# Normalised rows stored as two fp16 pieces and read back by transposing DMAs, in an attention and mixture-of-experts kernel on one core

## What is computed

```python
# x, ctx: 16 x 128 x 512, fp32.  D = 512 columns.
ln(x)  = (x - mean) / sqrt(var + 1e-5)
# cross attention per sample: 8 heads of 16 rows, over the 128 x 512 matrices
qk = einsum('hdq,hdl->hql', ln(x) heads, ctx heads) / 4
a  = einsum('hql,hdl->hdq', softmax(qk), ctx heads) * gamma
x1 = x + tanh(g_xattn) * a
u  = ln(x1)                                    # the "normalised rows"
# expert layer on u: 2048 tokens of 512
h = u @ down_w + down_b                        # 256 columns
logits = u @ router_w + router_b - cost        # 8 experts, the two best
out = sum over both of gate * (gelu(gelu(h) @ w1 + b1) @ w2 + b2)
out += 0.1 * (gelu(gelu(h) @ shared_w1 + shared_b1) @ shared_w2 + shared_b2)
out = out @ up_w + up_b + gelu(u) @ core_w + core_b
result = x1 + tanh(g_ffn) * out
```

## Time and profile before

| | |
|---|---|
| median of 3 runs | 705.38 us (704.84 to 709.47) |
| the profiled execution | 702.09 us, span 699.5 us from first to last instruction |
| busy share of the span | PE 94%, ACT 76%, DVE 73%, POOL 67% |
| chain that ended last, by engine | PE 65%, POOL 13%, DMA 11%, ACT 3%, DVE 3% |
| DMA | 120.40 MB, mean 172 GB/s |

### The profile page before, as it was taken

How to read it: one execution, slowest core, us unless ns; L and a number is a source line. 1 busy time by engine, 2 the same in 40 slices (tenths; PEclk the granted TensorE clock), 3 DMA queues, 4 the chain that set the end, 5 groups by cost and what they waited for, 6 DMA issues and landing times.

```text
span 699.5 us, 18429 instructions
## 1 busy us (share of the span) xinstructions
PE 655.4 (94%) x6005; PEld 344.4 (49%) x6005; DVE 512.5 (73%) x859; ACT 531.0 (76%) x1125; POOL 466.8 (67%) x468
## 2 busy tenths in 40 slices
PE   1799999999999999999999998879999999999998
PEld 0122222222222222222364554469889999998744
DVE  3989999999999999999779657554343343344466
ACT  2389999999999999999886747447677777777411
POOL 3698998988989888886658441405665665665722
PEclk9999999999999999999999999999999999999999
DMA  6655776666766666555254752459987997696596
GB/s 204 240 167 187 223 247 200 189 197 187 218 205 203 219 195 193 193 160 191 85 152 163 266 183 78 159 138 170 131 138 116 118 139 113 95 120 95 61 296 252
DMA packets 128482, 120.40 MB, mean 172 GB/s; under 512 B 64132, under 2 KB 97668, under 8 KB 128392
## 3 DMA queue, kind: packets, MB, share of 16 engines
q1 hardware_dynamic: 114968, 104.09, 51.7%
q0 software_dynamic: 12192, 14.16, 13.5%
q10 hardware_dynamic: 1232, 0.98, 0.5%
HBM read 60.25 MB, written 49.10 MB: 156 GB/s over the span
## 4 chain that ended last, share of the span: by engine, by line
PE 65%; POOL 13%; DMA 11%; ACT 3%; DVE 3%; issue 2%; SPq 1%; another core or an unknown queue 1%; POOLq 0%; DVEq 0%
PE EH L1333 24%; PE Y L1333 15%; PE pv L571 11%; PE ring L558 7%; PE nat L546 4%; ACT P L642 2%; DMA rd<-den_scratch 2%; DMA k_scratch<-khl 2%; POOL wlo L812 2%; DMA u<-in_wall 2%; DMA q_scratch<-qhl 1%; POOL tn L746 1%; POOL y_sums L2231 1%; POOL khl L804 1%; POOL whi L808 1%
## 5 line engine op out<-in xcount | busy, mean ns | idle before, releaser
L717 DVE TENSOR_REDUCE mx<-nat 128x2 f32<-128x1024 f32 x256 | 296.2, 1210 | 14.5 <-PE nat L546 14.3
L642 ACT ACTIVATE P<-ring 128x512 f32<-128x512 f32 x512 | 281.1, 601 | 16.2 <-PE ring L558 10.2
L2231 POOL DMA_INDIRECT y_sums<-ysb,to x74 | 123.2, 1665 | 92.5 <-DVE ysb L2165 73.6
L571 PE MATMUL pv<-P,VT 128*32 128x256 f32 x2048 | 157.9, 392 | 0.4
L546 PE MATMUL nat<-KS,QS 48*128 48x512 f16 x512 | 113.1, 395 | 21.1 <-DMA QS<-q_scratch 15.1
L558 PE MATMUL ring<-QS,KS 49*128 49x512 f16 x512 | 119.0, 391 | 8.0 <-ACT P L642 6.8
L1333 PE MATMUL EH<-XA,whi 128*128 128x256 f16 (+1 forms) x688 | 104.8, 258 | 0.0
L1333 PE MATMUL Y<-whi,u 128*128 x592 | 104.0, 273 | 0.1
L571 PEld LDWEIGHTS pv<-P,VT 128*32 128x32 f32 x2048 | 44.0, 108 | 99.3 <-issue 49.3
L2115 DVE TENSOR_TENSOR u<-X,u 128x512 f16<-128x512 f32 x62 | 42.6, 689 | 62.1 <-ACT u L1739 61.7
L1333 PE MATMUL EH<-XA,wlo 128*128 128x256 f16 (+1 forms) x344 | 84.7, 258 | 0.0
(11 more groups left out here) (282 smaller groups left out, 1029.3 us busy)
## 6 DMA issues: line engine op xcount, KB each, us to landing
QS<-q_scratch SPq DMA_DIRECT2D x64, 96.0 KB, 2.9
KS<-k_scratch SPq DMA_DIRECT2D x62, 96.0 KB, 2.3
u<-in_wall SPq DMA_DIRECT2D x7, 640.0 KB, 4.0
X<-in_x SPq DMA_DIRECT2D x16, 256.0 KB, 3.5
q_scratch<-qhl SPq DMA_DIRECT2D x16, 256.0 KB, 2.1
xr<-in_x SPq DMA_DIRECT2D x16, 256.0 KB, 3.4
rd<-den_scratch SPq DMA_DIRECT2D x16, 256.0 KB
u_rows<-un SPq DMA_DIRECT2D x16, 256.0 KB
```

The source lines that it names most:

```text
L571: m = pe.matmul(pv[32 * j:32 * j + 32, q], VT[i][:, lb, g, j, :], Pb[4 * (s % 2) + j][:, q], start=(lb == 0 and half == 0), stop=(lb == 3) ...
L642: act.activation(Pb[4 * (s % 2) + j][:, :], bank[:, :], ACT.Exp).then_inc(t_use.sem, 1)
L717: dve.tensor_reduce(mx[:, k // 8, :, k % 8], nat[k % 2][:, :, :], AX.X, ALU.max).then_inc(t_max.sem, 1)
L2231: pool.indirect_dma_start(out=ysum[:, :], out_offset=bass.IndirectOffsetOnAxis(ap=to[:, j % 2, a:a + 1], axis=0), in_=ysb[j % 2][:, a, :], ...
```

## The change

Attention now writes `u` as two fp16 pieces: after `u` (L766, into a spare buffer) GpSimd makes `uhi` and `ulo`, and SP stores both to a `u_rows` of two halves. `load_u(r)` becomes two transposing DMAs, of the high and of the low pieces, straight into the places that `h` reads: `uh` and `ul` for odd groups, the two halves of `XA` for even ones. `uT` (TensorE), `uT` and `uh` (ScalarE), `ul` (VectorE), the four casts `uhp` (GpSimd) disappear. `uf` is now the sum of both pieces, four adds on VectorE at the head of each body; `lg` and `gu` wait for it. `load_u(3)` moves from before the stores of group 0's residual rows to behind `sums(0)`, ahead of `load_x(2)`. The core of the diff:

```diff
--- before.py
+++ after.py
@@ -178,7 +179,7 @@
-    us = nc.dram_tensor("u_rows", [B, P, L], F32, kind="Internal").ap()
+    us = nc.dram_tensor("u_rows", [2, B, P, L], F16, kind="Internal").ap()
@@ -255,7 +258,8 @@
-    un = A("un", [P, L])
+    uhl = A("uhl", [P, 2, L], F16)
+    un = lambda b: gap[0][:, 0, :] if b < B - 3 else u[:, :, :].rearrange("p t q -> p (t q)")[:, UN_AT:UN_AT + L]
@@ -348,7 +352,7 @@
-            jobs += [(w - 3, n) for n in ("xnegm", "xveps", "xrstd", "u", "x1t")]
+            jobs += [(w - 3, n) for n in ("xnegm", "xveps", "xrstd", "u", "uhi", "ulo", "x1t")]
@@ -489,8 +493,8 @@
-                ck.wait(t_pool, s, "u")
-                sp.dma_start(us[s], un[:, :]).then_inc(t_us.sem, 16)
+                ck.wait(t_pool, s, "ulo")
+                sp.dma_start(us[:, s].rearrange("h p q -> p h q"), uhl[:, :, :]).then_inc(t_us.sem, 16)
@@ -762,8 +766,14 @@
+                done(pool.tensor_scalar(un(b), ao[i][:, :], lnx[:, 0:1], lnx[:, 2:3], ALU.add, ALU.mult))
+            elif what == "uhi":
+                ck.wait(t_pool, b, "u")
-                done(pool.tensor_scalar(un[:, :], ao[i][:, :], lnx[:, 0:1], lnx[:, 2:3], ALU.add, ALU.mult))
+                done(pool.tensor_scalar(uhl[:, 0, :], un(b), 1.0, 1.0, ALU.mult, ALU.mult))
+            elif what == "ulo":
+                ck.wait(t_pool, b, "uhi")
+                done(pool.tensor_tensor(uhl[:, 1, :], un(b), uhl[:, 0, :], ALU.subtract))
@@ -868,7 +878,7 @@
-        eng.wait_ge(t_pool.sem, t_pool.at[B + 1, "wlo"])
+        eng.wait_ge(t_pool.sem, max(t_pool.at[B + 1, "wlo"], t_pool.at[B - 4, "ulo"]))
@@ -961,9 +971,12 @@
-    xb, ub = [X, XB, X, XB], [XA, XA, u, XA]
+    xb = [X, XB, X, XB]
+    even = flat(XA).bitcast(F16).rearrange("p (h k q) -> p h k q", h=2, k=LB)
+    high_of = lambda r: uh[:, :, :] if r % 2 else even[:, 0]
+    low_of = lambda r: ul[:, :, :] if r % 2 else even[:, 1]
@@ -1025,17 +1038,17 @@
-                "pe": four("uT") + [("lg", 0), ("lt", 0), ("h", 0), ("h", 1), ("rk", 0), ("rt", 0), ("rt", 1), ("gt", 0), ("rt", 2), ("rt", 3)],
+                "pe": [("lg", 0), ("lt", 0), ("h", 0), ("h", 1), ("rk", 0), ("rt", 0), ("rt", 1), ("gt", 0), ("rt", 2), ("rt", 3)],
-                "dve": four("uf") + [("lpc", 0)] + four("ul") + R_(["lred", "lb", "lmx", "lsub", "lcl"] + route_a + route_s + route_p) +
+                "dve": four("uf") + [("lpc", 0)] + R_(["lred", "lb", "lmx", "lsub", "lcl"] + route_a + route_s + route_p) +
-                "pool": four("uhp") + four("sc"),
+                "pool": four("sc"),
-            ahead = cur(four("uT")) + older([("y", 1)]) + old([("a", 0), ("a", 1)]) + \
+            ahead = older([("y", 1)]) + old([("a", 0), ("a", 1)]) + \
@@ -1044,7 +1057,7 @@
-            ahead = cur([(n, k) for k in range(LB) for n in ("uT", "uh")]) + old([("a", 0), ("sah", 0)]) + cur([("lg", 0)]) + \
+            ahead = old([("a", 0), ("sah", 0)]) + cur([("lg", 0)]) + \
@@ -1052,7 +1065,7 @@
-            ahead = cur(four("ul")) + old([("sal", 0)]) + cur(R_(["lred", "lb", "lmx", "lsub", "lcl"] + route_a)) + low(0) + \
+            ahead = cur(four("uf")) + old([("sal", 0)]) + cur(R_(["lred", "lb", "lmx", "lsub", "lcl"] + route_a)) + low(0) + \
@@ -1174,11 +1183,14 @@
-            if r in (1, 3):
-                wait(sp, t_pe, (0, 0, 0, 1)[r], "uT", LB - 1)
-            elif r == 2:
-                sp.wait_ge(t_z.sem, 4)
-            sp.dma_start(ub[r][:, :, :], us[r * G4:(r + 1) * G4].rearrange("t p q -> p t q")).then_inc(t_uu[r % 2].sem, 16)
+            if r == 1:
+                ends["stacks"](sp)
+            elif r >= 2:
+                wait(sp, t_pe, r - 2, "h", 1)
+                wait(sp, t_dve, r - 2, "uf", LB - 1)
+            for h, dst in enumerate((high_of(r), low_of(r))):
+                rows_ = us[h, r * G4:(r + 1) * G4].rearrange("t p q -> (t p) q")
+                sp.dma_start_transpose(dst, rows_).then_inc(t_uu[r % 2].sem, 16)
@@ -1224,7 +1236,6 @@
-            load_u(3)
@@ -1245,6 +1256,7 @@
+                    load_u(3)
@@ -1368,28 +1379,20 @@
-                if name != "uT":
-                    wait(pe, t_act, 0, "uT", early[0, name, i])
-            if name == "uT":
-                if i == 0:
-                    wait(pe, t_uu[r % 2], r)
-                for t in range(G4):
-                    m = pe.transpose(dst[:, t * P:t * P + P], ub[r][:, t, i * P:i * P + P], ident)
-            elif name == "lg":
+            if name == "lg":
-                    wait(pe, t_act, r, "uT", k)
+                    wait(pe, t_dve, r, "uf", k)
+                if i == 0:
+                    wait(pe, t_uu[r % 2], r)
-                    if i == 0:
-                        wait(pe, t_act, r, "uh", k)
-                        wait(pe, t_dve, r, "ul", k)
-                    m = three(dst, slice(c0, c0 + P), uh[:, k, :], ul[:, k, :], k == 0, k == LB - 1)
+                    m = three(dst, slice(c0, c0 + P), high_of(r)[:, k, :], low_of(r)[:, k, :], k == 0, k == LB - 1)
@@ -1526,13 +1529,8 @@
-        def rows_0(lo, hi):
-            if lo == 0:
-                ends["scores"](pe)
-            for k in range(lo, hi):
-                do(0, "uT", k)
-
+            ends["scores"](pe)
@@ -1599,14 +1597,7 @@
-            if name == "uT":
-                wait(act, t_act, r - 1, "guh", i)
-                wait(act, t_dve, r - 1, "gul", i)
-                m = act.copy(uf[:, i, :], src)
-            elif name == "uh":
-                wait(act, t_pe, r - 1, "h", 1)
-                m = act.copy(uh[:, i, :], bank(r, "uT", i))
-            elif name == "lg":
+            if name == "lg":
@@ -1619,9 +1610,8 @@
-                wait(act, t_dve, r, "ul", i)
+                wait(act, t_dve, r, "uf", i)
-                wait(act, t_act, r, "uT", i)
@@ -1996,17 +1986,15 @@
-                wait(dve, t_pe, 0, "uT", i)
-                m = dve.tensor_copy(uf[:, i, :], bank(0, "uT", i))
+                if i == 0:
+                    wait(dve, t_uu[r % 2], r)
+                wait(dve, t_act, r - 1, "guh", i)
+                wait(dve, t_dve, r - 1, "gul", i)
+                m = dve.tensor_tensor(uf[:, i, :], high_of(r)[:, i, :], low_of(r)[:, i, :], ALU.add)
-            elif name == "ul":
-                wait(dve, t_act, r, "uT", i)
-                wait(dve, t_act, r, "uh", i)
-                wait(dve, t_pe, r - 1, "h", 1)
-                m = dve.tensor_tensor(ul[:, i, :], uf[:, i, :], uh[:, i, :], ALU.subtract)
```

More of the change, by code:

```diff
@@ L57 @@
 R_MAX = K_QK
+UN_AT = 2 * NT * 16
 HALF = 64
@@ L230, in attention @@
     wst = [v[:, :, :].rearrange("p t q -> p (t q)") for v in (XA, u)]
+    gap = []
     def stacks(i):
         if i:
-            A("gap", [P, 3, L])
+            gap.append(A("gap", [P, 3, L]))
         own = [A(f"{n}{i}", [P, 2, QUADS // 2, L], F16) for n in ("QS", "KS")]
@@ L518, in last_u @@
         def last_u():
-            sp.wait_ge(t_pool.sem, t_pool.at[B - 1, "u"])
-            sp.dma_start(us[B - 1], un[:, :]).then_inc(t_us.sem, 16)
+            sp.wait_ge(t_pool.sem, t_pool.at[B - 1, "ulo"])
+            sp.dma_start(us[:, B - 1].rearrange("h p q -> p h q"), uhl[:, :, :]).then_inc(t_us.sem, 16)
         late["sync"] = last_x1, last_u
@@ L832, in last_norm @@
         def last_norm():
-            for what in ("xnegm", "xveps", "xrstd", "u", "x1t"):
+            for what in ("xnegm", "xveps", "xrstd", "u", "uhi", "ulo", "x1t"):
                 job(Clock(pool), B - 1, what)
@@ L1070, in ffn @@
         t_xx[r % 2].plan(r)
-        t_uu[r % 2].plan(r)
+        t_uu[r % 2].plan(r, n=2)
         for t in range(G4):
@@ L1075, in ffn @@
             t_xs.plan(r, n=G4)
-    early = {(0, "uT", k): k for k in range(LB)}
-    early |= {(0, "lg", 0): 0, (0, "lt", 0): 1, (0, "h", 0): 2, (0, "h", 1): 3}
+    early = {(0, "lg", 0): 0, (0, "lt", 0): 1, (0, "h", 0): 2, (0, "h", 1): 3}
     moved = {(t_act, (0, "lg", 0)): (t_dve, (0, "lpc", 0))}
@@ L1086, in ffn @@
         moved[t_dve, o] = t_pool, o
-    for k in range(LB):
-        moved[t_act, (0, "uT", k)] = t_dve, (0, "uf", k)
-        moved[t_act, (0, "uh", k)] = t_pool, (0, "uhp", k)
     ring = []
     for o in [o for r in BODIES for o in seq("pe", r) if o not in early]:
-        if o[1] in ("uT", "lg", "lt", "h", "a", "gt", "core", "rk", "tot"):
+        if o[1] in ("lg", "lt", "h", "a", "gt", "core", "rk", "tot"):
             ring.append(o)
@@ L1262, in rest @@
             wait(sp, t_dve, NG - 1, "r", "ro")
-            wait(sp, t_pe, NG - 1, "uT", LB - 1)
+            wait(sp, t_pe, NG - 2, "h", 1)
+            wait(sp, t_dve, NG - 2, "uf", LB - 1)
             def all_rows_out():
@@ L1357, in read_out @@
                     wait(pe, t_act, q, "nz", 0)
-                elif name == "uT":
-                    wait(pe, t_act, q, "uh", i)
                 elif name == "gt":
@@ L1591, in rest @@
                 m.then_inc(t_pe.sem, 1)
[L1593 removed]
+        places = {(B - 1, "pv", 3): logits_0,
```

(19 more changed lines are left out.)

2 lines of the change are left out of this document (removed).

## The result

The changed kernel takes 718.89 us in the median of four runs (717.53 to 719.36); the kernel before, on the same chip, 705.11 us (703.22 to 709.47). The ratio is 1.0183, with a 95% interval of 1.0134 to 1.0232: the change costs 13.8 us.

The account below looks back on a forecast made before the run. Four engines were taken as nearly level in the attention windows, GpSimd with 1.04 us of room per window, and TensorE as setting the end later. 7.5 - 2.1 + 0.8 = +6.2 us on 705.38 gave 711.6 us, range 704 to 720.

Parts of the forecast that it names:

- Part 1: Attention windows from 3: two more GpSimd instructions per block, window 20.69 us; +7.5 us, ends +4 and +10.
- rival (c): Worse case: waits for rd and x_rows return each window, TensorE's clock drops in body 1; 718 us, chance 0.22.
- Part 2: Window 16: group 0's transposes leave TensorE and ScalarE's waits behind them go; -2.1 us.
- Part 3: Group bodies 1 to 3: transposes go, but logits need the uf adds; +1.9, -0.9, -0.2, together +0.8 us.
- Part 4: Transposing loads on SP's queue: no cost on the path, up to +2 us if cover fails.
- rival (d): Pauses without a releaser move with the instruction streams and may vanish or double; +-5 us on each case, no chance given.

Follow-up runs that it names:

- e2: Changed kernel without the GpSimd pair: u written as one fp16 piece, second piece zero; 713.60 us, ratio 1.0119.
- e4: Kernel before with the GpSimd pair alone added, its outputs read by nobody; 710.91 us, ratio 1.0077.
- e5: Changed kernel with group 1's loads issued behind xr and the logits taken from the two fp16 pieces; 707.45 us, ratio 1.0057.
- e7: Changed kernel with group 1's loads behind xr, logits from the pieces, and no GpSimd pair (11-bit rows); 699.94 us, ratio 0.9931.
- e1: Changed kernel with group 1's two transposing loads issued in window 16 behind the load of xr; 714.63 us, ratio 1.0122.
- e3: Changed kernel with the router's logits taken from the two fp16 pieces instead of uf; 714.64 us, ratio 1.0134.
- e8: Changed kernel with its eight transposing loads made plain loads of the same bytes; 712.52 us, ratio 1.0100.
- e6: e5 with the uf adds of bodies 1 to 3 moved behind gl(1) on VectorE; 703.24 us, ratio 0.9980.
- e9: e6 with GpSimd's output bias additions for blocks 0 to 11 moved from the attention windows to the group bodies; 706.13 us, ratio 1.0034.
- e11: e9 with the bias additions of groups 1 and 2 moved behind gl(0) of the next body; 708.05 us, ratio 1.0035.

## Why the prediction was right, and where its steps failed

The measured 718.9 us lie in the range and on the side forecast, 7.3 us above the point. By its steps:

**Part 1, the pair: right in mechanism and nearly in size.** It said 1.81 us per block, a window of 20.69 us and the start of window 14 at 305.2; the trace has 1.82 (256.78 to 258.60), 20.70 and 304.80. Waiting was absorbed to the last microsecond (12.5 to 1.3). At window 15 TensorE was 5.65 us late where 6.7 to 7.7 were said. For the +7.5 the medians give 5.3 us (e2), 5.7 (e4) and 7.5 (e5 against e7), all inside the ends 4 and 10. Two of the signs that were named came out weaker: GpSimd is busy for 93% of the stretch, not over 95, and TensorE waits for the query stack five times, not in most windows. The waits of rd and x_rows did not come back in windows 3 to 14, so that half of rival (c) is refuted; later the wait for rd in window 15 is 3.91 us where it was 1.79, and the one in window 16 is as before (7.93 and 7.94).

**Part 2, window 16: not seen.** The -2.1 us were to show in rt(0). In e7, which has none of the three costs, rt(0) stands 1.0 us behind before. A part of that is no matter of window 16: e7's GpSimd starts window 14, without a pair in it, at 298.32 us, 1.9 behind before's 296.43, and from there to rt(0) it takes 66.4 us against 67.2. So at most some 0.9 of the 2.1 us is seen. That the room was used up by the uf adds, which follow a wait for block 13's statistics as the step itself feared, is argued and not shown.

**Part 3, the bodies: right for 2 and 3, too small for 1.** For 2 and 3 the trace has -0.15 and -0.19 us against -0.9 and -0.2. For body 1 it said +1.9, and the trace has +5.39. The order "gul, adds, lg, h" was the right chain; its sizes were not. gul takes 4.64 us for four beside a busy GpSimd, 4.00 in the trace before (the step had gul end where ul starts today, at 371.4, 7.7 us behind rt(0); it ends 10.1 behind rt(0) after). lg, paced by the adds, takes 3.63 us instead of 1.17. And TensorE comes out of two pauses at the lower clock. The first is not the bodies' own: behind the 4.72 us wait for the tables the clock is 0.51 over 5.48 us, so by estimate 5.48 x 0.49 = 2.7 us are lost there, and e1, without that wait, has 2.2 us less in this stretch. That share of the 5.39 belongs to part 4. The second, behind the wait for the adds, is 0.69 over 3.56 us, by estimate 1.1 us. e3, which removes the dependence, gives 4.3 us in the median, over bodies 1 and 3. A clock drop in body 1 was in rival (c) with 1.7 us. The adds themselves are a little under their price, 2.48 us for four with two fp16 inputs and an fp32 output where 2.6 to 3.6 were said (5.05 and 5.07 in e1 and e7, where they and not gul fall beside GpSimd's work). At 2.48 they take as long as the four gul with fp32 inputs, 2.50: no doubled rate, as the Trainium skill has it under "Advanced Engine Details and Errata", "2x-1p Requirements", which asks for 16-bit input and output.

**Part 4, the loads: this step failed.** It costed them at nothing, with up to +2 if "rs, rd, cs2 and tabs queue behind them". That is what happened, in window 17 and with tabs as the last table to land, and it is 4.3 us by e1's reordering and 6.4 us by e8's plain form of all eight loads. The step took SP's time from one transposing DMA of 256 KB (1.37 us) and wrote 2.7 us per group; a group is four times 256 KB, so scaled by bytes that row gives 5.5, and 2.7 counts the two issues and not their size. It is 4.1 us in e1 and 7.0 us in window 17 of the changed kernel, where rd, u_rows and x_rows have been issued just ahead. It also looked at when the loads' own data is needed ("over 9 us before use") and not closely enough at what is issued behind them: the tables were already the last thing that the routing waited for.

The whole account: taken out together, the three costs are worth 19.0 us (e7), and with them out the change is worth 4.7 us against before; 19.0 - 4.7 gives back the 13.8 measured to 0.5 us, as it must, since all three are differences of the same medians. The prediction had 7.5 + 0 + 1.9 us of costs against 3.2 of gains. So the pair was sized right or oversized by some 2 us, the loads undersized by 4 to 6 us, and body 1 by 3.5 us in the trace, of which some 2 are the loads'; that the sum still fell into the range is owed to its upper end, which was rival (c)'s, and (c) had named the clock but not the loads. The pauses without a releaser of rival (d) are in nearly every build (5.1 to 5.9 us on VectorE ahead of the expert loop in before, after, e1 to e4, e7 and e8; 8.76 us on ScalarE in e6, with VectorE's gone). In e5 the same wait of VectorE, 5.83 us, is put down to a product of TensorE, so that it may be an ordinary wait whose releaser the trace misses. What places them stays open, and so does how much of e6's, e9's and e11's differences is theirs.

## What to carry to other kernels

Before adding an instruction per tile, compare its time with the engine's waiting per tile; beyond that it is paid, less the slack of what waits for the engine (8.4 us on GpSimd at window 14 were 5.65 on TensorE at window 15), and it stays to the end, however idle the engine looks by its share of the whole span. A DMA moved or changed in form is priced by what stands behind it on its issuing queue, not by its own landing, and its issue time has to be read under load. When an operand that arrived ready is now produced by another engine, look at whether its first consumer can take the raw pieces (e3, e6): with the loads moved and the logits taken from the pieces the change went from 1.8% slower to level with the kernel before.
